# A four-layer graph network on one core: the places of edges summed by TensorE, the tile list made by GpSimd, and the recurrent blocks' TensorE work woven across groups

## What is computed

```python
# third network, four blocks b; agg is a sum over the edges into each node
x = h * norm_src[:, None]
agg = segment_sum(x[src], dst)
g = agg * norm_dst[:, None] @ gcn_w[b] + gcn_b[b]
i_r, i_z, i_n = split(g @ gru_w_ih[b].T + gru_b_ih[b], 3)
r = sigmoid(i_r + h_r); z = sigmoid(i_z + h_z)
h = relu((1.0 - z) * tanh(i_n + r * h_n))
# fourth network: messages are summed by src, so the edges are regrouped by src
W = silu(rbf_ij @ W1 + b1) @ W2 + b2
agg = zeros.at[idx_i].add(h[idx_j] * W)
```

## Time and profile before

| what | value |
|---|---|
| runs shown | 6454.86 us median of 3 (6450.83 to 6454.93) |
| profiled execution | 6452.62 us, its span 6451.0 us |
| mean granted TensorE clock | 0.836 of 2.4 GHz |
| busy: PE, DVE, POOL, ACT | 4280.7, 3790.3, 3581.8, 1190.6 us |
| edge list stage | from about 7 to 144 us of the span |
| four recurrent blocks | from about 4507 to 5242 us |

### The profile page before, as it was taken

How to read it: one execution, slowest core, us unless ns; L and a number is a source line. 1 busy time by engine, 2 the same in 40 slices (tenths; PEclk the granted TensorE clock), 3 DMA queues, 4 the chain that set the end, 5 groups by cost and what they waited for, 6 DMA issues and landing times. The chain is left out here.

```text
span 6451.0 us, 102509 instructions
## 1 busy us (share of the span) xinstructions
PE 4280.7 (66%) x26702; PEld 2996.7 (46%) x26703; DVE 3790.3 (59%) x8560; ACT 1190.6 (18%) x1987; POOL 3581.8 (56%) x3658
## 2 busy tenths in 40 slices
PE   0666667385277777776366666663877778787884
PEld 0111114263156566665255555552545556565663
DVE  8777772154589899998466666665111235555553
ACT  0111111112211111111211122111211222222221
POOL 1222224502377777774277777760666667777772
PEclk9999999797589999998577766666988888988886
DMA  4000004200244444443233333335122222222233
GB/s 191 12 15 14 12 15 182 63 21 30 72 127 116 124 117 123 123 118 83 75 82 81 80 81 81 81 62 187 56 65 61 69 67 76 76 78 75 77 76 42
DMA packets 332968, 513.66 MB, mean 80 GB/s; under 512 B 104565, under 2 KB 245919, under 8 KB 322966
## 3 DMA queue, kind: packets, MB, share of 16 engines
q0 software_dynamic: 130656, 290.33, 17.9%
q1 hardware_dynamic: 202166, 221.78, 10.7%
HBM read 409.97 MB, written 101.86 MB: 79 GB/s over the span
## 5 line engine op out<-in xcount | busy, mean ns | idle before, releaser
L1027 POOL DMA_INDIRECT e_ring<-att_rows,e_near x1792 | 1839.6, 1027 | 550.3 <-issue 483.3
L1094 PE MATMUL e_psum<-e_ring,e_whole_pick 128*128 128x264 f32 (+1 forms) x3584 | 870.2, 397 | 301.7 <-DVE e_ring L1254 293.1
L1785 POOL DMA_INDIRECT e_nodes<-x,e_edges x832 | 814.6, 979 | 282.5 <-issue 263.0
L1094 PEld LDWEIGHTS e_psum<-e_ring,e_whole_pick 128*128 128x128 f32 x3584 | 667.7, 231 | 427.2 <-issue 192.1
L1049 PE MATMUL e_px<-t_parts,e_pick 128*128 x5376 | 700.4, 273 | 108.8 <-DVE e_pick L1156 51.5
L1172 DVE TENSOR_TENSOR e_prod<-e_px,e_ring 128x512 f32<-128x512 f32 x672 | 458.1, 682 | 486.3 <-DMA e_ring<-att_rows,e_near 390.5
L285 PE MATMUL b_acc<-b_pick_key,b_pick_lo 128*128 128x416 bf16 (+1 forms) x1960 | 498.1, 341 | 168.8 <-DVE b_pick_key L256 150.7
L1049 PEld LDWEIGHTS e_px<-t_parts,e_pick 128*128 128x128 bf16 x5376 | 459.3, 109 | 201.4 <-issue 130.5
L1701 POOL DMA_INDIRECT sorted<-rx_held,rx_index x432 | 425.3, 984 | 220.5 <-issue 210.4
L355 PE MATMUL r_pa<-gru_counts,gru_parts 128*128 x3000 | 449.6, 316 | 134.8 <-DMA r_bh<-in_gru_bh 95.8
L1136 ACT ACTIVATE e_whole_pick<-e_pturn 128x512 f32<-128x512 bf16 x448 | 266.6, 595 | 1324.8 <-PE e_pturn L1085 1297.9
(11 more groups left out here) (336 smaller groups left out, 6306.4 us busy)
## 6 DMA issues: line engine op xcount, KB each, us to landing
e_relb<-place SPq DMA_DIRECT2D x56, 1024.0 KB
e_ring<-att_rows,e_near POOLq DMA_INDIRECT x1792
sorted<-o_fill SPq DMA_DIRECT2D x11, 2508.0 KB
e_edges<-sorted SPq DMA_DIRECT2D x209, 132.0 KB
kept<-gin_counts SPq DMA_DIRECT2D x5, 4000.0 KB, 35.3
gru_counts<-kept SPq DMA_DIRECT2D x5, 4000.0 KB
rx_held<-in_edge_rows POOLq DMA_DIRECT2D x52, 297.0 KB
e_nodes<-x,e_edges POOLq DMA_INDIRECT x832
```

Of the source, the lines that this page charges most:

```text
L1027: pool.indirect_dma_start(out=ring[:, s, r, 0:wd + HEADS], out_offset=None, in_=xrows, in_offset=bass.IndirectOffsetOnAxis(ap=near[:, s, r ...
L1094: mm = pe.matmul(psum[q % 2][:, 0:RING], whole_pick[:, q % 2, c, :], ring[:, s, q * G + c, :], start=(c == 0), stop=(c == G - 1))
L1785: pool.indirect_dma_start(out=nodes[:, s, u, :], out_offset=None, in_=source, in_offset=bass.IndirectOffsetOnAxis(ap=edges[:, q, u, RBF + ...
```

## The change

In the edge list stage the sum over tiles goes to TensorE: for each t, two matmuls with the identity as weights add the two halves (391 columns, f32) of the masked `rank` into one PSUM tile `pslot`, each as soon as its mask is ready (`owned`). The tile list goes to GpSimd, as a compare and an add with a drain behind each, from the moment when `first` is ready (`ranged`). VectorE keeps the masks, and then only casts.

In the recurrent blocks TensorE's order is woven: the sums of half 0, the transposes of the group before, the graph product of half 0, the sums of half 1, the graph product of half 1, and the gate products half by half. The transposes now go to `pg[0]`. VectorE's group is unrolled in Python and takes the rows of the group before between the two scalings. An extra round of transposes, whose result nobody reads, stands in the first group.

```diff
                 with pe.Fori(0, NG) as g:
+                    sum_neighbours(pe, AT, parts, pa[0][:, 0:HW], 0, g, 0, split.lo).then_inc(sums, 1)
+                    turn(g - 1)
+                    convolve(g, 0)
+                    sum_neighbours(pe, AT, parts, pa[1][:, 0:HW], 0, g, 1, split.lo).then_inc(sums, 1)
+                    convolve(g, 1)
                     pe.wait_ge(taken, g * GT + 1)
                     for i in range(2):
-                        sum_neighbours(pe, AT, parts, pa[i][:, 0:HW], 0, g, i, split.lo).then_inc(sums, 1)
-                    for i in range(2):
-                        pe.wait_ge(sums_out, g * 2 + i + 1)
-                        pe.matmul(pg[2][i][:, 0:HW], wg[:, :], summed[:, halves[i]], start=True, stop=True).then_inc(convs, 1)
-                    pe.wait_ge(convs_out, g * 2 + 2)
-                    for c in range(GATES):
-                        for i in range(2):
+                        pe.wait_ge(convs_out, g * 2 + i + 1)
+                        for c in range(GATES):
                             pe.matmul(pg[c][i][:, 0:HW], wi[:, c * P:(c + 1) * P], conv[:, halves[i]],
                                       start=True, stop=True).then_inc(gates, 1)
-                    pe.wait_ge(state, g + 1)
-                    for u in range(GT):
-                        pe.transpose(pa[u // 4][:, u % 4 * P:(u % 4 + 1) * P], cand[:, u * P:(u + 1) * P],
-                                     K["identf"][:, :]).then_inc(turned, 1)
+                turn(NG - 1)
...
+                dve.sem_inc(state, 1)
+                for g in range(NG):
+                    scale_sums(g, 0)
+                    if g:
+                        take_rows(g - 1)
+                    scale_sums(g, 1)
+                    make_state(g)
+                take_rows(NG - 1)
...
+                pool.memset(tile[:, :], 0.0).then_inc(ready, 1)
+                pool.wait_ge(ready, 2)
+                pool.wait_ge(ranged, 1)
+                for t in range(1, NT):
+                    pool.tensor_scalar(past[:, :], count[:, :], first[:, t:t + 1], None, ALU.is_ge)
+                    pool.drain()
+                    pool.tensor_tensor(tile[:, :], tile[:, :], past[:, :], ALU.add)
+                    pool.drain()
+                pool.sem_inc(tiled, 1)
...
-                dve.drain()
+                dve.drain().then_inc(ranged, 1)
...
-                                             in1=own[:, t, :], op0=ALU.add, op1=ALU.mult)
-                dve.wait_ge(ready, 2)
-                for t in range(1, NT):
-                    dve.scalar_tensor_tensor(out=tile[:, :], in0=count[:, :], scalar=first[:, t:t + 1], in1=tile[:, :],
-                                             op0=ALU.is_ge, op1=ALU.add)
-                    dve.drain()
-                dve.tensor_reduce(slotf[:, :], rank[:, :, :].rearrange("p t c -> p c t"), AX_X, ALU.add)
+                                             in1=own[:, t, :], op0=ALU.add, op1=ALU.mult).then_inc(owned, 1)
+                dve.wait_ge(slotted, 1)
+                for h, lo, hi in parts:
+                    dve.tensor_copy(slot[:, lo:hi], pslot[:, h, 0:hi - lo])
+                dve.wait_ge(tiled, 1)
...
+                for t in range(NT):
+                    pe.wait_ge(owned, t + 1)
+                    for h, lo, hi in parts:
+                        mm = pe.matmul(pslot[:, h, 0:hi - lo], K["identf"][:, :], rank[:, t, lo:hi],
+                                       start=(t == 0), stop=(t == NT - 1))
+                mm.then_inc(slotted, 1)
```

More of the change, by code:

```diff
@@ L1479, in _ @@
                     for i in range(2):
-                        act.wait_ge(gates, g * 6 + i + 1)
+                        act.wait_ge(gates, g * 6 + i * GATES + 1)
                         act.activation(reset[:, halves[i]], pg[0][i][:, 0:HW], ACT.Sigmoid, bias=brz[:, 0:1]).then_inc(gates_out, 1)
-                    for i in range(2):
-                        act.wait_ge(gates, g * 6 + 3 + i)
+                        act.wait_ge(gates, g * 6 + i * GATES + 2)
                         act.activation(keep[:, halves[i]], pg[1][i][:, 0:HW], ACT.Sigmoid, bias=brz[:, 1:2], scale=-1.0).then_inc(gates_out, 1)
@@ L1499, in _, with scale_sums, make_state @@
                 dve.drain().then_inc(biases, 1)
-                with dve.Fori(0, NG) as g:
-                    for i in range(2):
-                        dve.wait_ge(sums, g * 2 + i + 1)
-                        dve.tensor_tensor(summed[:, halves[i]], pa[i][:, 0:HW], to_scale[:, ds(g * GW + i * HW, HW)],
-                                          ALU.mult).then_inc(sums_out, 1)
-                    dve.drain()
[L1506 to L1509, removed]
+                def scale_sums(g, i):
+                    dve.wait_ge(sums, g * 2 + i + 1)
+                    dve.tensor_tensor(summed[:, halves[i]], pa[i][:, 0:HW], to_scale[:, g * GW + i * HW:g * GW + (i + 1) * HW],
+                                      ALU.mult).then_inc(sums_out, 1)
+                def make_state(g):
+                    for i in range(2):
+                        dve.wait_ge(gates_out, g * 4 + i * 2 + 1)
+                        dve.wait_ge(gates, g * 6 + (i + 1) * GATES)
                         dve.scalar_tensor_tensor(out=cand[:, halves[i]], in0=reset[:, halves[i]], scalar=bh[:, 2:3],
@@ L1572, in edge_order @@
         tile = m.sb("o_tile", [P, NHALF])
+        past = m.sb("o_past", [P, NHALF])
         total = m.sb("o_total", [P, NT], I32)
@@ L1576, in edge_order @@
         offset = m.sb("o_offset", [P, NT])
-        slotf = m.sb("o_slotf", [P, NC])
         slot = m.sb("o_slot", [P, NSC], I32)
@@ L1581, in edge_order @@
         ppast, pall = (m.ps(f"o_p{n}", [P, BANK]) for n in ("past", "all"))
-        loaded, ready, filled, counted, summed, blank, listed, stored = (
-            m.sem(f"o_{n}") for n in ("loaded", "ready", "filled", "counted", "summed", "blank", "listed", "stored"))
+        pslot = m.ps("o_pslot", [P, 2, BANK])
+        loaded, ready, filled, counted, summed, owned, slotted, ranged, tiled, blank, listed, stored = (
+            m.sem(f"o_{n}") for n in ("loaded", "ready", "filled", "counted", "summed", "owned", "slotted", "ranged",
+                                      "tiled", "blank", "listed", "stored"))
+        parts = ((0, 0, NC // 2), (1, NC // 2, NC))
         with nc.Block() as block:
@@ L1609, in _ @@
                 pool.iota(count[:, :], pattern=[[1, NHALF]], base=0, channel_multiplier=0,
-                          allow_small_or_imprecise_dtypes=True).then_inc(ready, 1)
+                          allow_small_or_imprecise_dtypes=True)
+                pool.memset(tile[:, :], 0.0).then_inc(ready, 1)
[7 more added lines that the diff above has]
+                pool.sem_inc(tiled, 1)
             @block.vector
@@ L1614, in _ @@
                 dve.memset(ones[:, :], 1.0)
-                dve.memset(tile[:, :], 0.0)
                 dve.memset(src_tile[:, :], 0)
```

21 lines of the change are left out of this document (12 added, 9 removed).

## The result

The changed kernel takes 6468.96 us (median of 13 runs, 6463.23 to 6477.12), the one before 6454.86: ratio 1.0025, interval 1.0017 to 1.0033. I forecast 6440.7 and a range of 6424 to 6453; it is 28 us above the forecast, outside the range, and slower by a little more than the 0.2% that can be told. Its profiled execution took 6477.12 us, 24.5 more than that of before.

A forecast was written before the change was run, and what follows sets the result against it. VectorE alone was taken to bound the edge list stage, and GpSimd's sends to cap the recurrent blocks. Gains of 4.5 and 9.7 us, together 14.2, gave 6438.4 for the profiled execution and 6440.7 as median, range 6424 to 6453.

The forecast's parts named there:

- The compare's price: Edge list stage: a GpSimd compare of 416 columns takes 0.80 us, between 0.64 and 1.06.
- handles one stream: Edge list stage: reason to price the compare at 0.80 us, nearer the one-stream IOTA (0.64) than the two-input add (1.06).
- rival F: Edge list stage: GpSimd's compare costs several times the add, kernel slower than before, 6493 us at 3.0 a compare; chance 0.07.
- Turns: Edge list stage: VectorE masks and GpSimd list steps alternate, each instruction whole; 25 turns of 0.85 us cost GpSimd 21.3 us.
- Rival C: Edge list stage: GpSimd gets no turn until the masks are over, list ready at 143.9, kernel 6449 us; chance 0.15.
- TensorE at no cost: Edge list stage: TensorE's sum, 1.43 us a tile, ends at about 102, covered by GpSimd's later end, so costed at nothing.
- The blocks: Four recurrent blocks: weaving shortens TensorE's chain by about 24 us a block, but GpSimd's sends cap the gain at 9.7 in all.
- some 27: Recurrent blocks: a group takes some 27 us in the woven order, where it took 32.8.
- the 7 that I had set as a sign of being wrong: Recurrent blocks: the prediction is wrong if the four together shorten by more than 12 or less than 7 us.
- the fourth block's: Fourth recurrent block: gain of 5.3 us, the margin between SP at 5241.3 and GpSimd at 5236.0.

The follow-up runs named there:

- 64-column run: The kernel before with one compare of 64 columns on GpSimd in the edge list stage; ratio 0.9947 on the other chips, the compare taking 0.80 us.
- gru_only: The kernel before with only the recurrent blocks changed to the woven order, edge list stage as before; ratio 0.9978.
- pe_both_c: The changed kernel with the tile list put back on VectorE, third run; 6409.25 us, ratio 0.9928 to the kernel before.
- pool_part_d: The kernel before with only the tile list moved to GpSimd, reduction left on VectorE, old blocks; 6477.66 us, ratio 1.0033.
- edge_only: The kernel before with only the new edge list stage, recurrent blocks as before; ratio 1.0036.
- compares: The kernel before with 25 compares of 416 columns, each with a drain, on GpSimd, whose result nothing reads; ratio 0.9977 on the other chips.
- adds: The kernel before with 25 adds of 416 columns, each with a drain, on GpSimd, whose result nothing reads; ratio 0.9987 on the other chips.
- pe_part_b: The kernel before with only the sum over tiles moved to TensorE, list on VectorE, old blocks, run again; ratio 0.9953 on the other chips.

## Why the prediction was wrong

**The compare's price failed.** I took 0.80 us from a line through other operations; it is 1.32. The bounds that I gave, 0.64 and 1.06, did not hold it. The likeness that misled was "handles one stream": by the 64-column run some 0.7 us of a compare are there at any size. 24 x 0.52 is 12.5 us more. It stays below the 1.93 from which rival F's mechanism decides alone: the kernel came out slower, as F said, but not by F's way. The Trainium skill (GPSIMD Engine Reference, "Engine selection") puts one-input elementwise work roughly at line rate on GpSimd, from which I had estimated 0.35 us; this case's compare with a scalar from each partition takes 3.8 times that.

**Turns are real, but cheaper than I said.** I expected each list step to let one whole mask pass, 0.85 us, 25 times. In the trace a pair of steps takes 4.0 us while masks run (71.78 to 75.78) and 2.70 behind them, 1.3 more for a pair; the masks took 33.0 us instead of 23.68, 1.32 each and not 1.8, so that about three masks pass for every two steps. Nor is each instruction held up whole, as I had it: three masks of 0.95 and a pair of 2.70 would take 5.5 us one after the other, and they take 4.0. They partly run side by side, so blocking by the whole instruction, for which the prediction cites the Trainium skill (SBUF — State Buffer, "Who interferes with whom"), doesn't come out of this trace. The list as a whole: it started at 64.93 (forecast 64.5) and ended at 140.0 (135.0). Its 75.1 us are 57.1 of compares and adds (forecast 44.6), 7.7 of gaps of 0.16 behind each (4.6), and 10.3 left for turns (21.3). Two errors of opposite sign hid most of each other; the stage's gain is nothing instead of 4.5. Rival C, in which GpSimd gets no turn until the masks are over, puts the list's end at 142.9, the forecast at 135.0, the trace between them; but C's mechanism is refuted, as GpSimd was at work from 64.93 on.

**TensorE at no cost** was right: 100 passes in 35 us, 1.42 for a tile against 1.43 forecast, done at 102.

**The blocks were right in mechanism and nearly in size.** Groups of 26.4 us ("some 27"), GpSimd's drain last, and at about the old distance from the block's start: 4712.3 behind the start at 4533.4 is 178.9, before 180.0. The four blocks shortened by 8.2 us in this profile, 11.0 in the pair run again and 9.3 in `gru_only`, forecast 9.7. In `pe_both_c` it was 3.0 against `pool_part_d`, below the 7 that I had set as a sign of being wrong, and on the other chips 33 and more: the margins between GpSimd and SP, which I added up from one profile, are a thing of the chip and the execution. The term that was off is the fourth block's, 5.3 by its margin and 2.4 here: GpSimd itself came later there, 182.7 us into the block, where it was at 179.8 before. That need not be the weaving: in `edge_only`, with the old blocks, it came at 182.3.

**The step that was missing altogether** is what GpSimd's new work does to later stages: 14 to 18 us in the first attention's edge stage, through 896 gathers whose medians are 10 to 12 ns longer. I summed only stages that the change touches, and put all others at nothing without a reason. Shown are that the list on GpSimd brings it (`pool_part_d`) and moving the list back takes it away (`pe_both_c`), that work which nobody reads shifts the gathers as well, and, on the chips where before takes 6455 to 6459, the stage's answer. Open is the mechanism. That the operations leave something behind in GpSimd (L2) is one reading; that each kernel's later code comes to lie or load differently is another, and the sends, which one compare shifts in one stage and adds in five, go rather against a plain L2. That `compares` and `adds`, alike in the number of instructions, differ in the sends goes against a reading by the number alone. Open is also why the gathers of the second attention keep their 944 to 947 ns in every kernel. That another order of these operations, or other operations in between, takes it back, wasn't tried. The remaining lengthening of untouched stages, 14.4 and 6.7 us in the two executions of the changed kernel, is not settled either: between two executions of the kernel before these stages also differ by 5 us, but it is there in each pair of kernels with and without the list on GpSimd (13.3 from `pe_both_c` to `pool_part_d`).

The sum by its terms, for the profiled execution: edge list +0.3, blocks -8.2, first attention +17.9, the others +14.4, together +24.4, which is what the spans differ by. The forecast was -14.2. Of the 38.6 us between the two, the stages that I left out are 32.3, the edge list stage 4.8 and the blocks 1.5.

## What to carry to other kernels

Of two moves in one stage, look at each apart: here the one to an idle TensorE brought 33 us, and the one to an idle GpSimd took it all back, by turns with VectorE, by steps three times as dear (1.32 + 1.06 against 0.72 us), and by a cost in a stage 1600 us later. The gain from the weaving was 3 to 11 us where another engine was nearly as late, and 33 to 67 on chips where it wasn't: the margin between the last two engines belongs to the chip too. Before a fused VectorE step is split for GpSimd, time the very operation and size on it; a line through other operations missed a fixed part of 0.7 us. And when a change comes out worse than its stages say, lay the lengths of all stages side by side before looking closer at those that were changed.

## What the hardware showed

- A compare with a scalar from each partition on GpSimd took 0.80 us for 64 columns and 1.32 for 416; an add of two inputs 1.06 for 416.
- Beside VectorE's scans of 782 columns, compares alone took 1.88 us each in `compares`, where they take 1.32 undisturbed. Like the mask, the scan has two inputs (o_ones, o_own).
- Beside the masks, three masks and a pair of list steps took 4.0 us, where one after the other they would be 5.5.
- The four recurrent blocks with the old order took 734 to 737 us on the chips where before takes 6455 to 6459, and 765 to 807 on the others; in the woven order 726 to 731 and 725 to 731.
- Indirect gathers of one and the same code had a median of 946 to 949 ns or of 957 to 960 ns in the whole stage, by the kernel that they stood in; what differed was what GpSimd ran over a millisecond earlier. In all eight profiles of kernels with both operations it was the longer one, in all twelve without them the shorter. Indirect sends of another stage were at 969 to 971 instead of 958 to 962 also with one compare or with adds alone.
- On the chips where before takes 7330 us and more, the gathers' own instructions are no longer than elsewhere (946 ns in `pe_part_b`), but VectorE's product waits three times as long for its inputs, for releasers that the profile names "remote":

```profile
L1172 DVE TENSOR_TENSOR e_prod<-e_px,e_ring 128x512 f32<-128x512 f32 x448 | 305.9, 683 | 308.1 <-remote 164.0 <-PE e_px L1049 107.0 <-issue 29.1
```
